# Softmax sums of every first head moved from VectorE adds to one-column TensorE products, and four transpose buffers in the output phase

## The reference

```python
xn = _layernorm(x, axis=-1)
q = (xn @ Wq).reshape(b, s, 32, 128)
k, v = split(xn @ Wkv)
scores = einsum('bqhd,bkd->bhqk', q, k) * 128 ** -0.5
scores = where(causal, scores + slopes * (pos_k - pos_q), -inf)
s = einsum('bhqk,bkd->bqhd', softmax(scores), v).reshape(b, s, h) @ Wo
w = qweight * scales + scaled_zeros
g = silu(xn @ w.T + bias)
out = x + s * g
```

## Time and profile before

| what | value |
|---|---|
| median of three runs | 7741.44 us (7559.31 to 8016.49) |
| the profiled execution, its own time | 7566.46 us |
| its span on core 7, the slowest | 7564.8 us (cores: 7485.3 to 7564.8) |
| attention, four stages | 458, 481, 581 and 585 us |
| phase F | 347 us |

### The profile page before, as it was taken

How to read it: one execution, slowest core, us unless ns; L and a number is a source line. 1 busy time by engine, 2 the same in 40 slices (tenths; PEclk the granted TensorE clock), 3 DMA queues, 4 the chain that set the end, 5 groups by cost and what they waited for, 6 DMA issues and landing times.

```text
span 7564.8 us, 55969 instructions; the slowest of 8 cores (7485.3 to 7564.8 us)
## 1 busy us (share of the span) xinstructions
PE 4343.9 (57%) x18152; PEld 1760.2 (23%) x18152; DVE 2476.5 (33%) x2572; ACT 1831.9 (24%) x2712; POOL 1019.6 (13%) x787
## 2 busy tenths in 40 slices
PE   0000546765995220166566996986655669969910
PEld 0000212322443210011112443431111114434400
DVE  4443001110002442377675000006776780000012
ACT  6775000000002440034243000013553560000000
POOL 0000000000000000044253000003563660000000
PEclk9999988887997555577678998997787889989955
DMA  7777777767445889700001445540000003355588
GB/s 273 296 295 253 144 142 162 160 151 156 98 93 142 216 224 301 245 1 1 28 1 26 97 97 114 113 115 0 1 28 1 1 1 88 98 110 112 115 213 244
DMA packets 1553327, 936.99 MB, mean 124 GB/s; under 512 B 1331602, under 2 KB 1487250, under 8 KB 1520018
## 3 DMA queue, kind: packets, MB, share of 16 engines
q1 hardware_dynamic: 1243794, 648.17, 34.9%
q10 hardware_dynamic: 309248, 285.24, 12.5%
HBM read 581.01 MB, written 251.66 MB: 110 GB/s over the span
## 4 chain that ended last, share of the span: by engine, by line
PE 44%; DVE 22%; DMA 21%; ACT 6%; issue 3%; SPq 3%; POOL 1%; DVEq 0%; ACTq 0%; POOLq 0%
PE pbE L825 12%; PE pbE L775 12%; DVE accA L670 10%; PE pqC L476 9%; DVE rd_f L736 6%; DMA wqrC<-wq 4%; DMA wobh<-wobD 3%; DMA xA<-xkv 3%; DMA xcF<-xq 3%; DMA xntB<-xnh 3%; ACT wfoD L540 3%; PE pbE L731 3%; PE pbE L690 2%; DVE stA L301 2%; PE pbfD L560 2%
## 5 line engine op out<-in xcount | busy, mean ns | idle before, releaser
L476 PE MATMUL pqC<-xntqC,wqbC 128*128 128x512 bf16 x4096 | 939.3, 394 | 318.0 <-DVE wqbC L457 257.0
L670 POOL TENSOR_TENSOR accA<-accA,ppb 128x512 f32<-128x512 f32 x719 | 980.4, 1364 | 175.2 <-ACT ppb L715 52.3
L715 ACT ACTIVATE ppb<-pbE,bslE 128x512 bf16<-128x512 f32 x1264 | 791.6, 686 | 726.7 <-PE pbE L690 606.3
L825 PE MATMUL pbE<-attnTE,wftslE 128*128 128x512 bf16 x4096 | 889.3, 380 | 123.1 <-DMA wftslE<-wfth 122.1
L670 DVE TENSOR_TENSOR accA<-accA,ppb 128x512 f32<-128x512 f32 x681 | 873.6, 1283 | 226.7 <-ACT ppb L715 98.4
L775 PE MATMUL pbE<-attnTE,woslE 128*128 128x512 bf16 x4096 | 888.8, 380 | 18.9 <-DMA woslE<-wobh 18.9
L690 PE MATMUL pbE<-qtsE,kt 128*128 128x512 bf16 x1528 | 580.8, 437 | 380.7 <-DMA tsbE<-tstk 380.7
L665 POOL CAST accA<-ppb 128x512 f32<-128x512 bf16 x64 | 39.0, 610 | 5045.8 <-ACT ppb L720 3170.4
L659 PE MATMUL pbE<-ppb,vt 128*128 128x512 bf16 x1528 | 579.4, 404 | 193.6 <-ACT ppb L715 158.3
L380 PE MATMUL pbigB<-xntB,wkv_bf 128*128 128x512 bf16 x384 | 160.6, 418 | 885.7 <-DMA xntB<-xnh 879.6
L476 PEld LDWEIGHTS pqC<-xntqC,wqbC 128*128 128x128 bf16 x4096 | 410.5, 101 | 846.7 <-issue 400.3
(11 more groups left out here) (51 smaller groups left out, 2809.8 us busy)
## 6 DMA issues: line engine op xcount, KB each, us to landing
xA<-xkv SPq DMA_DIRECT2D x48, 2048.0 KB, 10.7
xnh<-xnA ACTq DMA_DIRECT2D x64, 1024.0 KB, 10.9
wqrC<-wq SPq DMA_DIRECT2D x32, 2048.0 KB, 18.7
qwD<-qw SPq DMA_DIRECT2D x32, 2048.0 KB, 9.7
worD<-wo SPq DMA_DIRECT2D x32, 2048.0 KB, 16.4
woslE<-wobh SPq DMA_DIRECT2D x64, 1024.0 KB, 8.9
wftslE<-wfth SPq DMA_DIRECT2D x64, 1024.0 KB, 9.3
xA<-xq SPq DMA_DIRECT2D x16, 2048.0 KB, 11.6
```

The lines of the kernel that those rows point to most:

```text
L476: mm_done = P.emit("tensor", lambda e, jj=j, c_=ch, p_=pb: e.matmul(pq[:, 2048 * p_ + 512 * c_:2048 * p_ + 512 * (c_ + 1)], wqb[p_][:, 128 ...
L670: ac = P.emit(eng, lambda e, pi=ppi_p, i_=i_p: e.tensor_tensor(out=accA[:, 512 * i_:512 * (i_ + 1)], in0=accA[:, 512 * i_:512 * (i_ + 1)], ...
L715: ex = P.emit("scalar", lambda e, b_=sb, pi=ppi, f_=fi, j_=j: e.activation(ppb[:, 512 * pi:512 * (pi + 1)], pb_[b_][:], AF.Exp, bias=bsl[: ...
L825: bb=bkf: e.matmul(pb_[bb + qq][:], wftsl[p_][:, 128 * g_:128 * (g_ + 1)], b_[:, c_ + 512 * qq:c_ + 512 * (qq + 1)], start=(g_ == 0), stop ...
```

## The change

Head 0's sum moves from VectorE to PE. In `flush_avd`, for head 0 of the pair, each AV product is followed by a product of the same exp tile with a bf16 column of ones, accumulated over the key tiles in row 0 of bank 6. VectorE has no cast and no add in the loop any more, head 0's L731 goes, and the reciprocal waits for the last of the new products. The exp of head 0 waits for the new product and not for an add. Head 1 stays as it was: GpSimd adds, then the fp32 product at the end.

In phase F sgt gets four buffers, and the transpose of tile t waits for the add of tile t - 4. The buffers of x and of the output, their waits and their order on ACT stay.

```diff
                                 waits=[("s", ex_p), bank_free[4 + i_p]], incs=[("t", 1)])
-                            eng, sn = (("vector", "v"), ("gpsimd", "g"))[i_p]
-                            if st_p:
-                                ac = P.emit(eng, lambda e, pi=ppi_p, i_=i_p: e.tensor_copy(
-                                    out=accA[:, 512 * i_:512 * (i_ + 1)],
-                                    in_=ppb[:, 512 * pi:512 * (pi + 1)]),
-                                    waits=[("s", ex_p), acc_guard[i_p]], incs=[(sn, 1)])
+                            if i_p == 0:
+                                ac = P.emit("tensor", lambda e, pi=ppi_p,
+                                            st_=st_p, sp_=sp_p: e.matmul(
+                                    pb_[6][0:1, :], c_onec[:, 0:1],
+                                    ppb[:, 512 * pi:512 * (pi + 1)], start=st_, stop=sp_),
+                                    waits=[acc_guard[0]], incs=[("t", 1)])
+                                last_ac[0] = ("t", ac)
+                                pp_free[ppi_p] = [("t", ac)]
                             else:
...
+                                if st_p:
+                                    ac = P.emit("gpsimd", lambda e, pi=ppi_p: e.tensor_copy(
...
+                                else:
+                                    ac = P.emit("gpsimd", lambda e, pi=ppi_p: e.tensor_tensor(
...
+                                last_ac[1] = ("g", ac)
+                                pp_free[ppi_p] = [("t", av), last_ac[1]]
...
                         h = heads[i]
-                        dmm = P.emit("tensor", lambda e, i_=i: e.matmul(
-                            pb_[6 + i_][0:1, :], c_onecf[:], accA[:, 512 * i_:512 * (i_ + 1)],
-                            start=True, stop=True),
-                            waits=[last_ac[i], bank_free[6 + i]], incs=[("t", 1)])
-                        acc_guard[i] = ("t", dmm)
+                        if i == 0:
+                            dmm = last_ac[0][1]
+                        else:
+                            dmm = P.emit("tensor", lambda e: e.matmul(
+                                pb_[7][0:1, :], c_onecf[:], accA[:, 512:1024],
...
-        sgt = [EF(nc.sbuf_tensor(f"sgtF{i}", [128, H], BF16)) for i in range(2)]
+        sgt = [EF(nc.sbuf_tensor(f"sgtF{i}", [128, H], BF16)) for i in range(4)]
...
-            pbu = t_ % 2
+            pbu = t_ % 4
             wv = [("v", lastF[pbu])] if pbu in lastF else []
+            wv2 = [("v", lastF2[t_ % 2])] if (t_ % 2) in lastF2 else []
```

More of the change, by code:

```diff
@@ L675, in flush_avd @@
-                            last_ac[i_p] = (sn, ac)
+                            if i_p == 0:
[6 more added lines that the diff above has]
+                                pp_free[ppi_p] = [("t", ac)]
+                            else:
+                                if st_p:
+                                    ac = P.emit("gpsimd", lambda e, pi=ppi_p: e.tensor_copy(
+                                        out=accA[:, 512:1024],
+                                        in_=ppb[:, 512 * pi:512 * (pi + 1)]),
+                                        waits=[("s", ex_p), acc_guard[1]], incs=[("g", 1)])
+                                else:
+                                    ac = P.emit("gpsimd", lambda e, pi=ppi_p: e.tensor_tensor(
+                                        out=accA[:, 512:1024],
+                                        in0=accA[:, 512:1024],
+                                        in1=ppb[:, 512 * pi:512 * (pi + 1)], op=ALU.add),
+                                        waits=[("s", ex_p), last_ac[1]], incs=[("g", 1)])
+                                last_ac[1] = ("g", ac)
+                                pp_free[ppi_p] = [("t", av), last_ac[1]]
@@ L676, in flush_avd @@
                             last_av[i_p] = av
-                            pp_free[ppi_p] = [("t", av), last_ac[i_p]]
                         pend.clear()
@@ L730, in build_nc @@
                         h = heads[i]
-                        dmm = P.emit("tensor", lambda e, i_=i: e.matmul(
-                            pb_[6 + i_][0:1, :], c_onecf[:], accA[:, 512 * i_:512 * (i_ + 1)],
-                            start=True, stop=True),
-                            waits=[last_ac[i], bank_free[6 + i]], incs=[("t", 1)])
-                        acc_guard[i] = ("t", dmm)
+                        if i == 0:
[3 more added lines that the diff above has]
+                                pb_[7][0:1, :], c_onecf[:], accA[:, 512:1024],
+                                start=True, stop=True),
+                                waits=[last_ac[1], bank_free[7]], incs=[("t", 1)])
                         rc = P.emit("vector", lambda e, i_=i: e.reciprocal(
@@ L857, in build_nc @@
         EF = stF.enter_context
-        sgt = [EF(nc.sbuf_tensor(f"sgtF{i}", [128, H], BF16)) for i in range(2)]
-        xcb = [EF(nc.sbuf_tensor(f"xcF{i}", [128, H], F32)) for i in range(2)]
-        osb = [EF(nc.sbuf_tensor(f"osF{i}", [128, H], F32)) for i in range(2)]
+        sgt = [EF(nc.sbuf_tensor(f"sgtF{i}", [128, H], BF16)) for i in range(4)]
+        xcb0 = [EF(nc.sbuf_tensor(f"xcF{i}", [128, H], F32)) for i in range(2)]
+        osb0 = [EF(nc.sbuf_tensor(f"osF{i}", [128, H], F32)) for i in range(2)]
+        xcb = xcb0 + xcb0
+        osb = osb0 + osb0
         lastF = {}
+        lastF2 = {}
         for t_ in range(16):
-            pbu = t_ % 2
+            pbu = t_ % 4
             wv = [("v", lastF[pbu])] if pbu in lastF else []
+            wv2 = [("v", lastF2[t_ % 2])] if (t_ % 2) in lastF2 else []
             d1_ = P.emit("sync", lambda e, tt=t_, p_=pbu: e.dma_start_transpose(
@@ L876, in build_nc @@
                 out=out[128 * tt:128 * (tt + 1), :], in_=osb[p_][:]),
-                waits=[("v", cv)], incs=[(f"fO{pbu}", 16)])
+                waits=[("v", cv)], incs=[(f"fO{t_ % 2}", 16)])
             lastF[pbu] = cv
+            lastF2[t_ % 2] = cv
         P.emit("sync", lambda e: e.nop(), waits=[P.dw("fO0"), P.dw("fO1")])
```

9 lines of the change are left out of this document (2 added, 7 removed).

## The result

The changed kernel is faster by 1.4%: the ratio of the times is 0.986, with a 95% interval of 0.982 to 0.991. That is about 106 us (72 to 139 by the interval), where 181 were forecast. It is clear of no change, but under the 2% that the prediction drew as its line: of its three outcomes it is "same", to which it gave 0.28. In the profiled execution of after, cores 0 to 3 show a mean clock of 0.81 and cores 4 to 7 one of 0.83, so I read core 7, as before.

The account below looks back on a forecast made before the run. It took DVE to bound pair ends, DVE and POOL together far loops, PE near loops. Pair ends -147, loops -31 and output phase -3 sum to -181 us, from 7566.46 to 7385 us; range 7300 to 7560.

Parts of the forecast that it names:

- same: Outcome for the whole kernel: a change of less than 2%, for which 151 us were needed; given 0.28.
- likeliest case: Whole kernel: the narrower span of 7330 to 7430 us around the forecast of 7385.
- I take 0.213: Price in us of each of 745 added one-column products on PE, as for 512-column bf16 products; 0.55 kept for the range.
- near pairs and pairs 6 and 7: Attention loops of the 24 near pairs (heads 0 to 11), +22 us, and of pairs 6 and 7, +10 us.
- other far pairs: Attention loops of far pairs from 12 tiles on: pace from 1.56 to 1.30 us a tile, 1.49 on the diagonal; -63 us.
- Rival A: PE in attention: the one-column product costs 0.55 us, so 142 of 181 us are gone, 7525; chance 0.19, whole or part.
- The end of a pair: After each pair's last exp: the reciprocal starts 0.3 us behind it, 2.3 us earlier, times 64: -147 us.
- POOL alone: Attention loops without DVE's adds: POOL's add takes 1.15 us, the next starts 1.30 after it, not 1.56.
- rival B: Far loops: POOL's add stays at 1.42 us and the pace at 1.56; 52 + 13 us of gain go, 7450; chance 0.11.
- Rival C: Far loops at ACT's pace, 1.16 to 1.20 us a tile; 7345 us; its chance is within the forecast's 0.66.
- Rival D: Attention loops: more PE work keeps PE at the half clock, +750 us for the whole, 7760 at half; chance 0.04.
- The output phase: Phase F with four transpose buffers: the load of xcF still ends last, only DMA traffic shifts; -3 us.

## Why the prediction was right or wrong

The sign was right and the size was not: 1.4% where 2.4% was forecast, 0.986 of 7566 is 7460 us where 7385 stood, inside the range but outside the likeliest case. The range reached to no gain at all, so lying in it says little.

**The step that failed** is "I take 0.213", for the one-column product. It measured 0.41. The reason given was that its nearest rows were the bf16 products of 512 columns; but what all of these have in common is weights 128 wide, and the rows with one column that the trace had (L731) were set aside as the farther relative. The trace of before even had such a place, at the end of each pair: the load of head 1's column (L731) starts with its product and 0.51 us after the product before it, in all 64 pairs, where full products at the half clock start 0.43 apart. It is a sign and no proof, since the product before it has one row of weights and the type changes too:

```profile
6119.84 0.58 PE L743 MATMUL pbE<-rd_b,c_oner 1*128 1x512 bf16 x1 [4.12 <-DVE rd_b L739]
6120.35 0.09 PEld L731 LDWEIGHTS pbE<-accA,c_onecf 128*1 128x1 f32 x2 [0.44 <-issue]
```

The sentence on the weight load, "hidden under the product before it as theirs are; uncovered it would be 0.08 to 0.1", names what happened, once for its own load and once more for the one behind it, which the bound did not count. The price went into two terms. In near pairs and pairs 6 and 7 the loops grew by 46.0 us, not 32. In the other far pairs they shrank by 29.6, not by 63: there the 1.71 of a diagonal tile, where 1.49 was forecast, is most of it, since away from the diagonal PE's five products at 1.28 come out level with POOL's 1.30. Kernels with 96 and 128 columns, in which nothing differs but the width of the ones, give some 80 us of attention back.

**Rival A** had the mechanism and the place, at 0.41 and not 0.55. I had said that the rule of the Trainium skill ("TensorEngine Tiling (Array Packing)", Key Properties: a change of mode needs TensorE to drain) would give A if a one-column load counts as such a change. The widths bear that out: dear up to 64 columns, not from 96, and paid per step and not per product, as a drain would be. That it is a drain of the array is argued from this pattern; no row shows it, and a load that is merely not started early would give the same pattern. (A's own sum has a slip: 181 less 142 leaves 39, which is 7527 and not 7525.)

**The end of a pair** was forecast at -147 and came to -130. The removed wait went in all 64 pairs; the reciprocal starts 0.54 us after the last exp in far pairs and 0.72 in near ones, where I had 0.3: the same 0.10 us steps, at the last ones products. With 96 columns it is 0.26 and 0.43, and the term -148.1.

**The tail** gave 13 us that no term had: head 1's fp32 product (L742) takes 1.87 us for its two passes behind head 0's part of the end, as L731 did in all 64 pairs of before, but in 20 pairs now 1.0 to 1.7; 1.02 is what L731 took in the earlier trace rows, right behind the loop. That is 12.5 of the 13 us. The 96-column kernel has the same 13.3, so it does not come with the width; that it comes with PE's being busier is argued and not shown.

**POOL alone** came out to the digit (1.15 and 1.30), so rival B is out. The lone add was the right row to trust, and the pair of engines at 1.56 shows how much they had slowed each other. Rival C is out as well: the 0.14 between POOL's adds stayed without DVE. In the changed kernel that pace is shared, since PE needs 1.28 there; with 96 columns, where PE has time to spare, it is still 1.30. Rival D did not come: the clock is 1.00 in the middle of the long loop, and the mean over the span rose from 0.824 to 0.833.

**The output phase** was forecast at -3 with -15 to +15 around it; the runs show nothing beyond the scatter between cores. Core 7's own 352 to 306 us is no effect of the change: without the new phase F the cores span the same 296 to 351, and with it cores 2 and 3 took 349 and 344. Core 7's whole 7564.8 to 7405.5 us, which would be near the forecast, owes 46 us to that.

Attention accounts for 50 of the 75 us by which the forecast was too large. The other 25 are less than the interval leaves open (72 to 139 us of gain, against 128 in attention). The stages that the change leaves alone do differ, phase C above all (core 7: 1257 us before from the end of B, 1274 after, core 2: 1251 and 1298), and other executions show as much scatter there without a cause that I could name.

## What to carry to other kernels

Price an operation by the row that shares what could cost, here the width of the weights among its neighbours, and if no row does, let the dearer bound weigh as much as the cheaper. A column of ones for sums should be 128 wide: it costs less than one column here and hands over the sums already spread over the partitions. When work leaves the end of a block, look next at which buffers the rest of it still holds: copying four banks out first was worth 482 us where moving head 1's sum to PE alone was worth none.

## What was unexpected of the hardware

- A product with 1, 32 or 64 weight columns among products with 128 costs 0.10 us more on the way in and 0.10 (0.12 for 64) on the way out, its load not lying beside the product before it; with 96 and 128 columns it costs nothing more, and two narrow ones in a row pay once.
- VectorE's reciprocal of 512 fp32 elements a row takes 3.34 us for one row and 3.36 for 128, from PSUM or from SBUF.
- VectorE's and GpSimd's adds, 0.69 and 1.15 alone, ran at one pair per 1.56 us together. The Trainium skill, "SBUF — State Buffer", section "SBUF: two separate sides", calls the ports that they share an exclusive lock; by my estimate that would give 1.84, one add after the other, and the measurement is less.
